# A four-stage token model on one core: embedding and first norm by groups of four tiles, cross-covariance attention with three batches in flight

## What is computed

```python
h = layer_norm(emb_word[input_ids] + emb_pos[:S][None], emb_ln_s, emb_ln_b)
for l in range(L):                                  # four layers
    q, k = heads(h @ Wq[l] + bq[l]), heads(h @ Wk[l] + bk[l])
    ...
    h = layer_norm(h + a @ Wo[l] + bo[l], ln1_s[l], ln1_b[l])
    f = jax.nn.gelu(h @ W1[l] + b1[l], approximate=False)
    h = layer_norm(h + f @ W2[l] + b2[l], ln2_s[l], ln2_b[l])
...
x = _layernorm(h, axis=-1)                          # cross-covariance attention, 8 batches of 256 tokens
q, k, v = (qkv[..., 0], qkv[..., 1], qkv[..., 2])
q = q / jnp.linalg.norm(q, axis=1, keepdims=True)
k = k / jnp.linalg.norm(k, axis=1, keepdims=True)
attn = jnp.einsum('bnhd,bnhe->bhde', q, k) * temp   # 24 x 24 for each of 8 heads, over the tokens
attn = jax.nn.softmax(attn, axis=-1)
y = jnp.einsum('bhde,bnhe->bnhd', attn, v).reshape(b, n, c)
h = h + y @ W_proj + b_proj
...
gate_logits = jnp.einsum('bte,en->btn', _layernorm(h), Wg) + bg    # four experts
top = jnp.argmax(gate_logits, axis=-1)
```

## Time and profile before

| what | before |
|---|---|
| median of three runs | 1875.44 us |
| span of the profiled execution | 1874.5 us |
| PE busy, share of the span | 1483.1 us, 79% |
| DVE | 1247.8 us, 67% |
| ACT | 977.2 us, 52% |
| POOL | 808.0 us, 43% |

### The profile page before, as it was taken

The page is one execution under the profiler, slowest core; times in us unless marked ns, Lnnn a source line. Parts: engine busy times, 40 slices in busy tenths (PEclk is TensorE's granted clock), DMA queues, the critical chain, the costliest instruction groups (busy, mean ns, idle before and its releaser), DMA issues.

```text
span 1874.5 us, 42615 instructions
## 1 busy us (share of the span) xinstructions
PE 1483.1 (79%) x13098; PEld 1235.0 (66%) x13098; DVE 1247.8 (67%) x3542; ACT 977.2 (52%) x2392; POOL 808.0 (43%) x1177
## 2 busy tenths in 40 slices
PE   0589889798897997998988759759668887499992
PEld 0367678677676776776767648449646766389992
DVE  4788966788767888668896652433379896434344
ACT  0378733688434885348873223225348882155550
POOL 6577333684235762247733310124356521144440
PEclk9899989899899997999998968669869996599996
DMA  4666101743005550035610000147534511257765
GB/s 105 176 149 127 36 1 33 170 86 84 1 5 138 108 121 2 1 70 140 128 33 1 1 14 1 45 138 224 173 89 100 112 22 45 97 175 237 225 212 179
DMA packets 144317, 178.26 MB, mean 95 GB/s; under 512 B 22096, under 2 KB 106128, under 8 KB 143952
## 3 DMA queue, kind: packets, MB, share of 16 engines
q1 hardware_dynamic: 136784, 158.18, 32.9%
q0 software_dynamic: 7296, 17.18, 2.8%
HBM read 132.96 MB, written 42.34 MB: 94 GB/s over the span
## 4 chain that ended last, share of the span: by engine, by line
PE 31%; DVE 14%; issue 4%; DMA 2%; ACT 2%; POOL 2%; SPq 0%; DVEq 0%; POOLq 0%; ACTq 0%
PE bank L1473 7%; DVE ptl L799 4%; PE bank L1459 2%; DVE neg_max L792 2%; PE bank L645 1%; DVE xn L912 1%; PE bank L563 1%; PE bank L1460 1%; PE bank L1463 1%; PE bank L1461 1%; PE bank L1462 1%; PE bank L1217 1%; DMA xn<-y_rows 1%; PE bank L431 1%; PE bank L584 1%
## 5 line engine op out<-in xcount | busy, mean ns | idle before, releaser
L685 ACT ACTIVATE prob<-bank,neg_max 128x192 f32<-128x192 f32 (+1 forms) x960 | 406.9, 437 | 109.3 <-DVE neg_max L792 97.0
L792 DVE TENSOR_REDUCE neg_max<-bank 128x2 f32<-128x384 f32 (+1 forms) x480 | 274.3, 572 | 99.0 <-PE bank L544 91.4
L799 DVE TENSOR_TENSOR ptl<-bank,pth 128x384 f16<-128x384 f32 (+1 forms) x480 | 275.5, 574 | 4.6 <-ACT pth L698 4.0
L563 PE MATMUL bank<-ident,prob 128*128 128x128 f32 x1536 | 268.4, 288 | 0.0
L698 ACT ACTIVATE pth<-bank 128x384 f16<-128x384 f32 (+1 forms) x480 | 244.3, 509 | 9.3 <-PE bank L563 9.2
L652 ACT ACTIVATE xx<-bank 128x256 fp32r<-128x256 f32 x256 | 95.5, 386 | 196.0 <-PE bank L431 192.0
L544 PE MATMUL bank<-kx,qx 96*128 96x192 bf16 (+1 forms) x960 | 168.1, 257 | 1.1 <-DVE xx L766 1.1
L563 PEld LDWEIGHTS bank<-ident,prob 128*128 128x128 f32 x1536 | 162.9, 143 | 0.1
L584 PE MATMUL bank<-v,pth 128*128 128x33 bf16 x1152 | 138.4, 180 | 21.2 <-DVE ptl L799 18.0
L645 PE MATMUL bank<-w,fbuf 128*128 128x192 f32 x768 | 140.7, 327 | 2.0 <-DVE h L889 2.0
L734 ACT ACTIVATE fbuf<-bank,b 128x512 f32<-128x512 f32 x96 | 65.8, 687 | 146.5 <-PE bank L453 146.4
(11 more groups left out here) (295 smaller groups left out, 4522.5 us busy)
## 6 DMA issues: line engine op xcount, KB each, us to landing
xn<-in_e_seg SPq DMA_DIRECT2D x34, 768.0 KB
w<-in_e_w SPq DMA_DIRECT2D x23, 576.0 KB
qk_rows<-fbuf SPq DMA_DIRECT2D x128, 96.0 KB, 2.3
qx<-qk_rows SPq DMA_DIRECT2D x35, 288.0 KB, 4.0
kx<-qk_rows SPq DMA_DIRECT2D x35, 288.0 KB, 5.8
qk_rows<-w SPq DMA_DIRECT2D x80, 96.0 KB, 2.3
qx<-qk_rows SPq DMA_DIRECT2D x35, 192.0 KB, 4.6
kx<-qk_rows SPq DMA_DIRECT2D x35, 192.0 KB, 5.2
```

Source lines behind the costliest of these rows:

```text
L563: last = nc.tensor.transpose(bank[BT[p % 2]][:, c * P:c * P + P], probs_at(p, banded, c * P, P), ident[:, :])
L685: nc.scalar.activation(probs_at(p, banded, qt * n, n), scores_at(p, n)[:, qt, :], ACT.Exp, bias=neg_max[:, b % 2, hd, qt:qt + 1], scale=1. ...
L792: nc.vector.tensor_reduce(neg_max[:, b % 2, hd, :], scores_at(p, D if banded else S), AX.X, ALU.max, negate=True).then_inc(max_ready.sem, 1)
L799: nc.vector.tensor_tensor(ptl[:, p % 2, 0:n], bank[BT[p % 2]][:, 0:n], pth[:, p % 3, 0:n], ALU.subtract)\
```

## The change

At the start the token ids are loaded first, places and window go to scratch in `prob` and the mask's values to `fbuf`, so that `hb` is free. The gathers count on a semaphore for each group; POOL does the gathers of groups 0 and 1, the first power, the weights, the second power, the gathers of groups 2 and 3, then waits for all of them. DVE works group by group, and the first turns and chunks come between. POOL's 12 `hb` sums follow after v and `middle`. The fill of scratch rows moves to the last layer's attention.

In the cross-covariance stage the input norm goes into the last layer's tail by groups, and the turns of batches 0 and 1 into PE's steps 19 and 22. The probabilities are multiplied by the projection first (`m`), then by v (`o`): there is no transpose of the probabilities and one product less. POOL adds the squares of a batch's two tiles, so that there are half as many one-column products. The loop has batch i in its gram, batch i - 1 in its softmax and products and batch i + 2 in its turn; the second norm and the gate, now token by token with no transposed logits, are in it too.

```diff
+            sp.dma_start(tok[:, :], a["x"]).then_inc(tok_in.sem, 16)
...
-            sp.dma_start(tok[:, :], a["x"]).then_inc(tok_in.sem, 16)
...
@@ POOL, start
+            gather(0)
+            gather(1)
+            pool_rstd(pool, ch, 0, 1 - NG, 0, 1e-12)
...
             pool_weights(ch, wa, QKV).then_inc(wa_ready.sem, 1)
...
+            pool_rstd(pool, ch, 0, 2 - NG, 1, 1e-12)
+            gather(2)
+            gather(3)
             pool_ones(ch)
+            for g in range(NG):
+                pool.wait_ge(gathered[g].sem, 16 * GT)
+            pool_rstd(pool, ch, 0, 3 - NG, 2, 1e-12)
+            pool_v(pool, ch, 0, 0)
+            pool_middle(pool, ch, 0, 0)
+            pool_middle(pool, ch, 0, 1)
+            pool_rstd(pool, ch, 0, 4 - NG, 3, 1e-12)
+            for g in range(NG - 1):
+                first_sums(g)
@@ DVE, start
+            embed(0)
+            first_norm(0)
             for kind, i in OPENING:
+                if (kind, i) == ("chunk", 0):
+                    embed(1)
+                if (kind, i) == ("v", 0):
+                    first_norm(1)
+                    embed(2)
                 dve_open(dve, ch, 0, kind, i, True, first_split(0))
+            embed(3)
+            first_norm(2)
@@ dve_tail, last layer (cross)
+                if cross:
+                    if g >= 2:
+                        dve_xc_normalise(dve, g - 2)
+                    if 1 <= g < NG:
+                        dve_xc_stats(dve, ch, g - 1)
+                    if g == NG - 1:
+                        dve_xc_split(dve, 0)
+                        dve_xc_split(dve, 1)
@@ under
+            steps = {3 * FC + 1: lambda: last(0), 3 * FC + 4: lambda: last(1)} if last else {}
+        def pe_xc_x(pe, b):
+            if b >= 2 and gated(b - 2) is not None:
+                pe.wait_ge(gx_ready.sem, 2 * gated(b - 2) + 2)
+            pe.wait_ge(xn_ready.sem, xn_ready.at(0, 2 * b + 2))
+            pe.wait_ge(xx_ready.sem, xx_ready.at(L, b))
...
+        def pe_cross(pe):
...
+            for i in range(B + 3):
+                g = gated(i)
+                if i < B:
+                    pe_xc_gram(pe, i)
+                if 1 <= i <= B:
+                    pe_xc_m(pe, i - 1)
+                if g is not None:
...
+                    pe_gate_x(pe, g, 0, min(B, i + 2))
+                if i + 1 < B:
+                    pe_xc_qk(pe, i + 1, 0)
+                if 1 <= i <= B:
+                    pe_xc_o(pe, i - 1)
+                if g is not None:
+                    pe_gate(pe, g, 0)
+                    pe_gate_x(pe, g, 1, min(B, i + 2))
+                if i + 1 < B:
+                    pe_xc_qk(pe, i + 1, 1)
+                if g is not None:
+                    pe_gate(pe, g, 1)
+                if i < B:
+                    pe_xc_turn(pe, i)
+                if i + 2 < B:
+                    pe_xc_x(pe, i + 2)
+                if i + 1 < B:
+                    pe_xc_v(pe, i + 1)
...
+        def dve_cross(dve, ch):
+            for i in range(B + 2):
+                if 1 <= i <= B:
+                    dve_xc_logits(dve, ch, i - 1)
+                    dve_xc_probs(dve, ch, i - 1)
+                if i < B:
+                    dve_xc_norms(dve, i)
+                    dve_xc_keys(dve, ch, i)
+                if i == 0:
+                    dve_affine(dve, ch, L - 1, NORMED.index((2, NG - 1)) + 1, NG - 1, 1)
...
+                if i >= 3 and i % 2:
+                    g = (i - 3) // 2
+                    dve_normalise(dve, ch, L, NG + g + 1, g)
+                if 1 <= i <= B:
+                    dve_xc_out(dve, i - 1)
+                if i + 2 < B:
+                    dve_xc_split(dve, i + 2)
+                if 1 <= i <= B and i % 2 == 0:
+                    dve_stats(dve, ch, 0, 1, i // 2 - 1, xc_o_ready)
```

More of the change, by code:

```diff
@@ L257, in build_tower @@
         tok_in = sig("tok_in", base=0)
-        gathered = sig("gathered", base=0)
+        gathered = [sig(f"gathered_{g}", base=0) for g in range(NG)]
         tok_ok = sig("tok_ok", base=0)
@@ L516, in early_steps, with under @@
             return list(zip(at, OPENING))
-        def under(turn, out=None, first=None):
-            steps = {}
+        def under(turn, out=None, first=None, last=None):
+            steps = {3 * FC + 1: lambda: last(0), 3 * FC + 4: lambda: last(1)} if last else {}
             for g in range(NG - 1):
@@ L914, in dve_normalise @@
                 last.then_inc(xn_ready.sem, 1)
[L916 to L925, removed]
         def dve_affine(dve, ch, it, n, g, w):
@@ L988, in pool_rstd, with pool_hb @@
                 .then_inc(rstd_ready.sem, 1)
-        def pool_hb(pool, it, n, g, row):
-            for t in range(GT * g, GT * g + GT):
+        def pool_hb(pool, it, n, g, row, tiles=range(GT)):
+            for t in [GT * g + i for i in tiles]:
                 pool.wait_ge(h_ready.sem, h_ready.at(it, n + t % GT))
@@ L1184, in pe_xc_gram @@
                     nc.tensor.matmul(o[0:96, c], qkt(b, i)[:, ck], qkt(b, i)[:, c], start=(i == 0), stop=(i == 1))
[L1185 to L1188, removed]
+            pe.wait_ge(xc_sq_ready.sem, xc_sq_ready.at(0, b + 1))
+            for s in range(2):
+                for at, first in ((D + s, D), (D + 2 + s, 0)):
+                    last = nc.tensor.matmul(o[0:96, at:at + 1], sqt(0)[:, first + 96 * s:first + 96 * s + 96],
+                                            xc_one[:, 0:1], start=True, stop=True)
             last.then_inc(xc_gram_done.sem, 1)
@@ new lines, in dve_xc_stats @@
+        def dve_xc_stats(dve, ch, g):
+            c = []
+            for t in range(GT * g, GT * g + GT):
+                dve.wait_ge(h_ready.sem, h_ready.at(L - 1, normed(2, t)))
+                c.append(ch.mark(nc.vector.bn_stats(stats[:, (t + NT - GT) % NT, :], h[:, t, 0:D])))
+            for t in range(GT * g, GT * g + GT):
+                ch.done(c[t - GT * g])
+                alone(dve)
+                last = nc.vector.bn_aggr(mv[:, t, :], stats[:, (t + NT - GT) % NT, :])
+                if t < GT * g + GT - 1:
+                    ch.mark(last)
+            last.then_inc(xc_mv_ready.sem, 1)
@@ new lines, in dve_xc_logits @@
+        def dve_xc_logits(dve, ch, b):
+            if b == 0:
+                dve.wait_ge(aux_in.sem, 16 * 8)
+            ch.done(xc_scaled[0])
+            dve.wait_ge(xc_kt_done.sem, xc_kt_done.at(0, b + 1))
+            for s in range(2):
+                last = ch.mark(nc.vector.scalar_tensor_tensor(
+                    xc_s[0:96, 0, s, :], in0=bank[6 + b % 2][0:96, 256 + 96 * s:256 + 96 * s + 96],
+                    scalar=xc_small[0:96, 0, s:s + 1], in1=xc_mask[0:96, s, :], op0=ALU.mult, op1=ALU.add))
+            ch.done(last)
```

421 lines of the change are left out of this document (224 added, 197 removed).

## The result

The changed kernel took **1826.52 us** (median of four runs, 1819.72 to 1826.94), the kernel before, run on the same chip, 1874.84 (1871.28 to 1877.36): a ratio of 0.9737, with a 95% interval from 0.9715 to 0.9759. Forecast was 1824, range 1804 to 1845. The span of the profiled execution is 1823.3 us, 51.2 under that of before; lines in the new numbering are a few higher (L1967 for L1736, L891 for L889, and so on).

The account below looks back on a forecast made before the run. PE was taken to bound the loop, with waits for ACT and DVE; at the start PE waits on a chain. 1874.5 - 14 (start) - 37 (gate) = 1823.5 us, median 1824, range 1804 to 1845.

Parts of the forecast that it names:

- 14 + 37: Sum of both gains: 14 us from the start, 37 at the gate, with the layer-end loss already taken off.
- Start, 14 forecast: Kernel start: ids and gathers sooner, ACT's next chunk waiting for POOL's pieces; gain 14 us, bounds 7 and 18.
- The gathers' landing: Start: the later eight gathers at 1.58 us each, issued by 49, landed by 52; bounds 49.5 and 61.
- The layer's end, 13 forecast: Last layer: PE stands about 8 us for DVE's split, products end near 1081; loss 13 us, bounds 8 and 17.
- The first `m`: From the last layer's products to the loop's first `m`: about 17 us, so 1098.
- The cycle: Cross-covariance loop: chain and PE's work nearly tie, clock stays mixed; seven cycles about 77 us, intervals 11 to 12.
- The tail: Behind the last `m`: o, residual, last group's norm, turns and gate products take 14 us, gate at 1189.
- The gathers were not starved: Rival at the start: DVE holds later gathers up, POOL's pieces come at 86, start gain 7, 1831 us; chance 0.14.
- The clock was not full: Rival: PE never falls to 1.2 GHz in the loop, gathers run unhindered; start 18, stage 47, 1810 us; chance 0.14.
- Cycles of 14 to 15: Rival: the loop overlaps little, a late m holds all behind it; 1837 to 1844 us; chance 0.14.
- 19.4: Slower rival: loop cycle from which the kernel is no faster; batches in step take 20.4 us, 1882; chance 0.02.
- the strict reading of the forecast: Start: port rule holds each of the later eight gathers behind DVE's norm and pieces, giving the first rival's 1831 us.

## Why the prediction was right

The sum was 14 + 37; at the gate it was 9.9 + 36.5 (9.9 is the shift of PE's step 19, 1052.93 to 1043.04, just ahead of the cross stage). That the profiled span still shows 51 is owed to the 4.8 us behind the gate, which no step named. By the medians it is 48.3. The mechanisms held, but part of the agreement is luck: in the stage the layer's end came 1.6 us under its forecast and the first `m` 2.6 under, the tail 3.8 over, and these cancel.

- *Start, 14 forecast, 9.9 in this profile.* The mechanism was right (ACT's chunk waits for POOL's pieces), some sizes were not. The affine, put at 4.3, took 6.6 (25.35 to 31.95, beside POOL's weight splits, see the last section). From its end to the chunk it was 4.1, not 3, and the mask ended at 20.7, not 20.0; so the second power ended at 40.1, not 36.7. The gathers' landing, put at 52, was 57.4: they began 3.6 later, took 13.2 in place of 12.6 (one of them 3.53), and landed 3.9 behind the last one, not 2.8. `v` and `middle` took 14.5, not 13.3, and the 12 sums 7.0, the lower end of 7 to 10. (The listed terms put POOL's first piece at 75.6 to 78.6, not at 77 to 79; it came at 82.05.) But this execution is the latest of six with the same start: the last layer's first activation stands at 981.7 here, at 976.6 to 979.7 in the five others, and at 991.3 and 991.7 in the two profiles with the old start. So the start gives 10 to 15 us there, and 14 is not shown to be too high.
- *The layer's end, 13 forecast.* PE stood 8.42 us (8 forecast) and the products ended at 1069.70; without the start's 9.9 that is 11.4 after their old end. One group earlier the split costs next to nothing there (77.2 us from the last layer's first activation, 76.5 with the old tail): 10.8 us, shown.
- *The first `m`* came 14.4 us behind the products' end, not 17: POOL's power and squares (1072.54 to 1074.99) ran beside DVE's norm (1072.26 to 1075.05), and the last affine took 3.5, not 4.5.
- *The cycle.* Seven took 77.3 us (77 forecast), a mean of 11.0 at a clock of 0.82; only the mean is as forecast, since single ones went from 7.1 to 14.7, not from 11 to 12. PE waits 1.3 to 3.0 ahead of `m` in seven of eight, so the chain as put is what it waits for there. In the cycles with the gate's products its own work is what counts: in the run with the softmax ahead such a cycle took 12.7 with PE busy 11.99.
- *The tail* from the last `m` to the gate was 17.8, not 14: PE's products there ran at the lower clock (from 1164 to 1175 it was 0.66, and the last `m` took 1.59, not 0.89).
- *The rivals.* The gathers were not starved: five of the later eight took 0.95, three of them beside DVE's pieces and norms; the first two took 1.40 and 1.38, each with one of DVE's one-input casts (0.43) inside. The clock was not full (0.82). Cycles of 14 to 15 came once in seven, and none was near 19.4.

On the rule for gathers beside DVE: the seventh gather ran from 14.15 to 16.37, the DVE operation beside it to 16.26 (DVE's and POOL's timelines of the changed kernel):

```profile
14.15 2.22 POOL L1967 DMA_INDIRECT h<-in_L_tok_emb_word,au  x1 [0.31 <-issue]
```

```profile
15.03 1.23 DVE L2140 TENSOR_SCALAR fbuf<-xn 128x2048 f32<-128x2048 f32 x1
```

So it holds for these wide operations with one input, 0.11 us behind their end. Beside the sums with two inputs (L2143) a gather took 1.06. The Trainium skill, SBUF — State Buffer, section "SBUF: two separate sides", puts two-input operations of DVE in conflict only with GpSimd operations that read SBUF, which the trace bears out (1.06 here, and in the last section 1.48 beside POOL's two-input splits for what takes 0.34), and the strict reading of the forecast was wider than that.

## What to carry to other kernels

When work is moved under another engine's stretch, look up what it waits for on the in-order engine that feeds it: here one split, one group too late in DVE's program, held up the last products and cost 10.8 us beside the 48 gained, and moving two lines gave them back. When a wait in a loop of four in-order engines is taken away, follow the next one on every engine ahead of changing the order: moving all norms behind the softmax took PE's wait ahead of `m` and made POOL's squares late instead. Measure such edits at a landmark right behind the stage, since unchanged stages behind it vary by more than the edit, and over several profiles: ACT's chunk at the start stood 2.5 us apart in six executions of the same start.

## What was not expected of the hardware

POOL's weight splits slow DVE's affine. In the changed kernel's timelines of POOL and DVE:

```profile
27.21 1.61 POOL L1030 TENSOR_TENSOR wa_lo<-raw,wa_hi 128x576 fp32r<-128x576 f32 x1 [0.18 <-POOL wa_second L1028]
28.79 1.43 POOL L1031 TENSOR_TENSOR wa_second_lo<-raw,wa_second 64x576 fp32r<-64x576 f32 x1
```

```profile
27.49 1.48 DVE L929 SCALAR_TENSOR_TENSOR h<-hb,rstd,ln_b 128x128 f32<-128x128 f32 x1
28.89 1.48 DVE L932 SCALAR_TENSOR_TENSOR h<-hb,rstd,ln_b 128x128 f32<-128x128 f32 x1
30.29 0.34 DVE L929 SCALAR_TENSOR_TENSOR h<-hb,rstd,ln_b 128x128 f32<-128x128 f32 x1
```

An operation that takes 0.34 us alone took 1.48 beside them, and ended 0.15 behind each; that is some 3 us on the way to the first chunk. The single gathers of about 3.5 us (3.46 before, 3.53 after) don't fall on such an operation of DVE and were not explained: whether the DMA queues held them up wasn't tried. And the clock's level in a stretch with short waits differs between executions: the stretch ahead of the gate ran at 0.77 in the profile of before and at 0.50 in that of the start alone, with the same products.
